# Spikes added inside TensorE's transposes, first tile pushed ahead, early norms on ScalarE

## The reference, cut to what matters

```python
h = layernorm(x) * (1 + ca) + sa
# per token: inp = r * wkv;  mem = 0.3*mem + inp - 0.05*(mem > 0.05);  spike = (mem - 0.05 > 0)
x = x + ga * spikes                       # "the sums"
h = layernorm(x) * (1 + cb) + sb          # 16 tiles of 128 tokens
for layer in range(2):                    # attention + MLP
    s = concat(h[:, :64], shift_by_one_token(h[:, 64:]))     # "shift_token"
    q, k, v = split(s @ wqkv[layer])
    q = q / max(norm(q), 1e-12) * q_scale   # per head, 8 heads of 64
    k = k / max(norm(k), 1e-12) * k_scale
    q, k = rotary(q), rotary(k)
    h = h + local_attention(q, k, v) @ wo[layer]             # window 64
    h = h + mlp(layernorm(shift_token(h)))
x = x + gb * h
```

## Time and profile before

| what | us |
|---|---|
| median of 3 runs | 548.56 (548.49 to 548.58) |
| profiled execution | 549.87, its span 548.1 |
| PE busy | 494.0 (90%) |
| DVE busy | 427.0 (78%) |
| ACT busy | 349.6 (64%) |
| POOL busy | 339.3 (62%) |

### The profile page before, as it was taken

One profiled execution on the slowest core, in us unless ns is written; L12 is line 12 of the kernel. 1 busy time (PEld: TensorE's weight loads), 2 busy tenths in 40 slices (PEclk: granted clock), 3 DMA queues, 4 the chain that ended last, 5 costly groups with the idle time before them and its releaser, 6 DMA issues.

```text
span 548.1 us, 11812 instructions
## 1 busy us (share of the span) xinstructions
PE 494.0 (90%) x4059; PEld 315.8 (58%) x4059; DVE 427.0 (78%) x1173; ACT 349.6 (64%) x1001; POOL 339.3 (62%) x271
## 2 busy tenths in 40 slices
PE   5844088999999999999899999999999999999996
PEld 5424033567777776443467777777544445667775
DVE  6999999899888976566889988995545687566665
ACT  5854007699999987534679999998556526533332
POOL 5990028999999998668989999994111277410000
PEclk9975579999999999999989999999999999999999
DMA  8600003211111112000221111111000000000000
GB/s 300 238 1 1 0 3 109 56 39 32 40 40 41 41 39 71 0 2 0 77 49 35 37 41 39 41 40 31 1 1 0 0 1 1 1 1 19 22 20 19
DMA packets 15025, 20.98 MB, mean 38 GB/s; under 512 B 2379, under 2 KB 9013, under 8 KB 14709
## 3 DMA queue, kind: packets, MB, share of 16 engines
q1 hardware_dynamic: 14676, 20.13, 13.3%
q10 hardware_dynamic: 288, 0.08, 0.1%
HBM read 9.99 MB, written 1.05 MB: 20 GB/s over the span
## 4 chain that ended last, share of the span: by engine, by line
PE 68%; DVE 18%; POOL 6%; issue 4%; ACT 3%; DMA 1%; DVEq 0%; SPq 0%; POOLq 0%; ACTq 0%
PE psT L1523 11%; PE psQK L1615 9%; PE psO L1738 6%; PE psO L1670 5%; PE psQK L1945 5%; PE psS L1718 5%; DVE vst L1108 3%; DVE vAB L1112 3%; PE psO L1523 3%; PE psS L2017 3%; PE psQK L1752 3%; PE psO L2017 2%; PE psQK L1877 2%; PE psS L1854 2%; PE psQK L1756 2%
## 5 line engine op out<-in xcount | busy, mean ns | idle before, releaser
L576 ACT ACTIVATE prob<-psS,nmx 128x128 f32<-128x128 f32 x256 | 90.1, 378 | 18.2 <-DVE nmx L1248 18.2
L904 POOL TENSOR_TENSOR rn<-ssq,half 128x16 f32<-128x16 f32 x32 | 93.2, 2913 | 8.6 <-DVE ssq L1234 8.5
L896 POOL TENSOR_TENSOR ra<-ra,rb 128x512 f32<-128x512 f32 x64 | 81.0, 1286 | 1.0 <-DVE rb L1216 0.8
L716 POOL TENSOR_TENSOR rst<-mv,half 128x4 f32<-128x4 f32 x24 | 25.7, 1072 | 73.8 <-DVE mv L1009 64.2
L1615 PE MATMUL psQK<-wqkv,hsA 128*128 128x512 f32 x128 | 62.0, 604 | 1.0 <-DVE hsA L1197 0.6
L576 ACT ACTIVATION_READ_ACCUMULATOR prob<-psS,nmx 128x1 f32 x256 | 55.4, 216 | 0.0
L912 POOL TENSOR_TENSOR qkn<-ra,rn 128x512 f32<-128x512 f32 x32 | 49.0, 1532 | 2.5
L1213 DVE TENSOR_TENSOR ra<-psQK,rope 128x512 f32<-128x512 f32 x64 | 43.9, 686 | 7.5 <-PE psQK L1615 6.6
L1216 DVE TENSOR_TENSOR rb<-psQK,rope 128x512 f32<-128x512 f32 x64 | 43.5, 680 | 0.0
L697 ACT ACTIVATE gel<-psQK 128x512 f32<-128x512 f32 x32 | 19.1, 597 | 37.5 <-PE psQK L1945 37.5
L1227 DVE TENSOR_REDUCE ssq<-sq 128x8 f32<-128x512 f32 x64 | 41.1, 676 | 1.6 <-ACT sq L516 1.3
(11 more groups left out here) (263 smaller groups left out, 1177.6 us busy)
## 6 DMA issues: line engine op xcount, KB each, us to landing
vAB<-vAB SPq DMA_DIRECT2D x62, 128.0 KB, 2.2
wqkv<-in_wqkv SPq DMA_DIRECT2D x2, 768.0 KB, 8.2
big<-in_x SPq DMA_DIRECT2D x4, 256.0 KB, 5.3
ra<-in_rope_t SPq DMA_DIRECT2D x1, 1024.0 KB, 7.7
ropeb<-in_rope SPq DMA_DIRECT2D x1, 1024.0 KB, 8.6
big<-in_ew SPq DMA_DIRECT2D x2, 512.0 KB, 4.1
wmod<-in_wmod SPq DMA_DIRECT2D x2, 384.0 KB, 6.8
out<-big SPq DMA_DIRECT2D x3, 256.0 KB, 2.3
```

The lines of the kernel that those rows point to most:

```text
L576: act.activation(prob[:, k, :], psS[:, hb, c * P:(c + 1) * P], ACT.Exp, bias=nmx[:, k:k + 1], accum_out=sums[:, n % 2, k:k + 1]).then_inc( ...
L896: pool.tensor_tensor(o, o, rb[:, r], ALU.add).then_inc(s["sum_" + name], 1)
L904: pool.tensor_tensor(rn[:, :], ssq[:, :], half[:, :], ALU.pow).then_inc(s["rn_ready"], 1)
```

## The change

1. Three currents on DVE: group 1's moves from POOL to DVE, before `quotient(3)`.
2. The spikes get a place of their own (`spikes = big[:, 6]`, where `x` had been loaded). PE transposes `x_cm` without them during the recurrence, and later adds the transposed spikes by a product with the identity into the same banks. `x_cm` itself gets them on POOL after the whole of layer 0's attention. The experts' weights, which go to the same place, are fetched at the start of layer 1.
3. In group 0 the first 128 tokens go ahead: one transpose, one scaling, two short copies. The other 384 tokens reach `hsA` by two transfers.
4. The inverse root of the first norm (group 0) and of attention tiles 0 and 1 is `exp(-0.5*ln(x))` on ACT; the activation table set is `natural_log_exp_and_others` for layer 0.
5. The lists of ACT, DVE, PE and POOL around it are reordered.

```diff
-                act.activation(rsg[:, gsl(g)] if g in (1, 2) else r_bank(g), ...
+                act.activation(rsg[:, gsl(g)] if g == 2 else r_bank(g), ...
+            act.preload_act_table_set("natural_log_exp_and_others")
             load_table(ACT.Exp)
...
+            def power(dst, src):
+                own.one(act.activation(dst, src, ACT.Ln, bias=0.0, scale=1.0))
+                return act.activation(dst, dst, ACT.Exp, bias=0.0, scale=-0.5)
+            def first_norm():
+                n = ln_no(1, 0)
+                act.wait_ge(s["ln_var"], n + 1)
+                power(rst[:, n % 4, :], mv[:, n % 4, :, 1]).then_inc(s["rst_act"], 1)
+                act.wait_ge(s["rst_act"], 1)
+                act.wait_ge(s["ln_rstd"], n + 1)
+                act.wait_ge(s["ln_t2"], n - 1)
+                for k in range(TPG):
+                    act.activation(lnx[:, n % 2, k, :], stat_bank(n)[:, k, :], ACT.Identity, ...).then_inc(s["ln_norm"], 1)
+                    if k == 1:
+                        act.wait_ge(s["first_t2"], 1)
+                        act.activation(z[:, 0:P], psQK[:, 0, 0:P], ACT.Identity, ...).then_inc(s["first_out"], 1)
+                act.wait_ge(s["ln_t2"], n + 1)
+                act.activation(z[:, P:GW], out_bank(n)[:, P:GW], ACT.Identity, ...).then_inc(s["ln_out"], 1)
+            def norms(n):
+                act.wait_ge(s["ssq_max"], n + 1)
+                if n:
+                    act.wait_ge(s["k_ready"], n)
+                    act.wait_ge(s["q_ready"], n)
+                power(rn[:, :], ssq[:, :]).then_inc(s["rn_ready"], 1)
-            ln_norm(ln_no(1, 0))
-            stack_out(0)
+            first_norm()
             ln_norm(ln_no(1, 1))
+            squares_k(0)
             ln_norm(ln_no(1, 2))
             stack_out(1)
-            squares_k(0)
             squares_q(0)
+            norms(0)
             ln_norm(ln_no(1, 3))
...  (ACT, tile -2: after k_turned)
+                    if n == 1 - LEAD:
+                        norms(1)
...  (POOL)
-            current(1)
             current(2)
-            add_spikes(2)
-            ln_rstd(ln_no(1, 0))
-            add_spikes(3)
-            for g in range(1, NG):
-                ln_rstd(ln_no(1, g))
+            n = ln_no(1, 0)
+            pool.wait_ge(s["rst_act"], 1)
+            pool.tensor_tensor(nmr[:, n % 4, :], nmean[:, n % 4, :], rst[:, n % 4, :], ALU.mult).then_inc(s["ln_rstd"], 1)
+            ln_rstd(ln_no(1, 1))
+            ln_rstd(ln_no(1, 2))
...
-                    norms(n + 2)
+                    if n + 2 > 1:
+                        norms(n + 2)
...
                     rope_sum(n + 3, 1)
+                    if n + 3 == 0:
+                        ln_rstd(ln_no(1, 3))
                     rope_sum(n + 3, 0)
...
                 if l == 0:
+                    pool.wait_ge(s["spikes"], 2)
+                    for g in range(NG):
+                        pool.tensor_tensor(x_cm[:, gsl(g)], x_cm[:, gsl(g)], spikes[:, gsl(g)], ALU.add).then_inc(s["x_mixed"], 1)
                     phase_scalars()
                     phase_whole()
...  (DVE)
             current(0)
+            current(1)
             quotient(3)
             current(3)
...
-            add_spikes(0)
-            add_spikes(1)
+            dve.memset(cend[:, 0, 0:1], 0.0).then_inc(s["spikes"], 1)
+            dve.tensor_scalar(by_chunk(spikes, NG - 1), of_group(ph, NG - 1, 1), -1.0, ...).then_inc(s["spikes"], 1)
             ln(ln_no(1, 0))
-            threshold(Steps(dve, s["spk"]), 3)
             ln(ln_no(1, 1))
-            ln(ln_no(1, 2))
...
-            dve.wait_ge(s["ln_out"], ln_no(1, 0) + 1)
-            shifted(hsA, z, 0, "hsA_ready")
+            dve.wait_ge(s["first_out"], 1)
+            dve.tensor_copy(hsA[0:64, 0:P], z[0:64, 0:P]).then_inc(s["hsA_first"], 1)
+            dve.tensor_copy(hsA[64:128, 1:P + 1], z[64:128, 0:P]).then_inc(s["hsA_first"], 1)
+            ln(ln_no(1, 2))
+            dve.wait_ge(s["rope_ready"], 4)
+            rope_products(0, 1)
             ln(ln_no(1, 3))
-            dve.wait_ge(s["rope_ready"], 4)
-            qk_first(0)
+            rope_products(0, 0)
+            sum_squares(0, 1)
+            sum_squares(0, 0)
+            clamped(0)
             rope_products(1, 1)
+            q_normed(0)
             rope_products(1, 0)
-            q_normed(0)
...  (PE)
+            for g in range(NG):
+                for k in range(TPG):
+                    mm(stat_flat(ln_no(1, g))[:, k * P:(k + 1) * P], x_cm[...], ident[:, :],
+                       is_transpose=True, start=(k == 0), stop=(k == TPG - 1), skip_group_check=True)
...
             def stack_t1(g):
-                pe.wait_ge(s["x_mixed"], g + 1)
-                four(stat_flat(ln_no(1, g)), lambda k: x_cm[...]).then_inc(s["ln_t1"], 1)
+                pe.wait_ge(s["spikes"], 1 + (g == NG - 1))
+                for k in range(TPG):
+                    i = mm(stat_flat(ln_no(1, g))[:, k * P:(k + 1) * P], spikes[...], ident[:, :],
+                           start=False, stop=(k == TPG - 1), skip_group_check=True)
+                i.then_inc(s["ln_t1"], 1)
             stack_t1(0)
             stack_t1(1)
             stack_t1(2)
-            keep_clock(10, psT1[:, :])
-            ln_t2(ln_no(1, 0))
             stack_t1(3)
+            keep_clock(2, psT1[:, :])
+            first = ln_no(1, 0)
+            pe.wait_ge(s["ln_norm"], TPG * first + 1)
+            pe.transpose(psQK[:, 0, 0:P], lnx[:, first % 2, 0, :], ident[:, :]).then_inc(s["first_t2"], 1)
             keep_clock(4, psT1[:, :])
             pe.wait_ge(s["ld_wq"], 16)
             pe.wait_ge(s["edges"], 4)
             proj_part(0, 0, 1)
+            pe.wait_ge(s["ln_norm"], TPG * (first + 1))
+            for k in range(1, TPG):
+                i = pe.transpose(out_bank(first)[...], lnx[:, first % 2, k, :], ident[:, :])
+            i.then_inc(s["ln_t2"], 1)
+            proj_part(0, 0, 0)
             ln_t2(ln_no(1, 1))
-            proj_part(0, 0, 0)
+            proj_part(0, 1, 1)
             ln_t2(ln_no(1, 2))
-            proj_qk(0, 1)
+            proj_part(0, 1, 0)
             keep_clock(4, psT1[:, :])
...  (SP)
+                    sp.wait_ge(s["ln_out"], ln_no(1, 0) + 1)
+                    sp.dma_start(hsA[0:64, P:GW], z[0:64, P:GW]).then_inc(s["hsA_dma0"], 16)
+                    sp.dma_start(hsA[64:128, P + 1:GW + 1], z[64:128, P:GW]).then_inc(s["hsA_dma0"], 16)
+                else:
                     sp.wait_ge(s["x_mixed"], NG)
                     sp.dma_start(ew1, a["ew1"]).then_inc(s["ld_ew"], 16)
                     sp.dma_start(ew2, a["ew2"]).then_inc(s["ld_ew"], 16)
```

More of the change, by code:

```diff
@@ L128, in program @@
         seed, rsg = ek, sab
+        spikes = big[:, 6, :]
         oT = big[:, 0:4, :]
@@ L189, in program @@
         names = """ld_id ld_x0 ld_x1 ld_x2 ld_x3 ld_wm0 ld_wm1 ld_ew ld_c ld_wr ld_wa ld_wq ld_wl ld_lru ld_rt ld_moe ld_out st_out
-            init table edges mod_raw cnt_ready cnt_sum renewed spk hsA_dma1 hsA_dma2 hsA_dma3 silu_c mod_mm mod_fin sc_ready
+            init table edges mod_raw cnt_ready cnt_sum renewed spikes hsA_dma0 hsA_dma1 hsA_dma2 hsA_dma3 silu_c mod_mm mod_fin sc_ready
             ln_t1 ln_var ln_rstd ln_norm ln_t2 ln_out
@@ L463, in receptance @@
                 act.wait_ge(s["num_ready"], min(g + 2, NG))
-                act.activation(rsg[:, gsl(g)] if g in (1, 2) else r_bank(g), r_bank(g), ACT.Sigmoid, bias=vec[:, V_BR:V_BR + 1]).then_inc(s["r_ready"], 1)
+                act.activation(rsg[:, gsl(g)] if g == 2 else r_bank(g), r_bank(g), ACT.Sigmoid, bias=vec[:, V_BR:V_BR + 1]).then_inc(s["r_ready"], 1)
             act.preload_act_table_set("natural_log_exp_and_others")
@@ L543, in v_copy @@
                 elif n == 0:
-                    act.wait_ge(s["x_mixed"], NG)
+                    act.wait_ge(s["spikes"], 2)
                 act.activation(vB[:, u, :], psO[:, 1, :], ACT.Copy).then_inc(s["v_evac"], 1)
@@ L1147, in threshold @@
             def threshold(steps, g):
-                steps.did(dve.tensor_scalar(by_chunk(ekv, g), of_group(ph, g, 1), -1.0, mod[:, 0, GA, bof(g):bof(g) + 1],
+                steps.did(dve.tensor_scalar(by_chunk(spikes, g), of_group(ph, g, 1), -1.0, mod[:, 0, GA, bof(g):bof(g) + 1],
                                             ALU.is_lt, ALU.mult))
+            dve.wait_ge(s["xT_evac"], NG)
             threshold(own, 0)
@@ L1590, in _ @@
                 mixer_turn(g)
-            pe.wait_ge(s["cur_vec"], 2)
+            pe.wait_ge(s["cur_vec"], 3)
             for n in range(4):
@@ L1601, in stacked @@
                 g = i // TPG
-                if l == 0 and g or g == NG - 1:
+                if l == 0 and i == 0:
+                    pe.wait_ge(s["hsA_first"], 2)
+                elif l == 0 or g == NG - 1:
                     pe.wait_ge(s[f"hsA_dma{g}"], 32 * (l + 1))
                 else:
-                    pe.wait_ge(s["hsA_ready"], 2 * (l + g + 1))
```

(18 more changed lines are left out.)

30 lines of the change are left out of this document (16 added, 14 removed).

## The result

The changed kernel takes 551.92 us (median of 5, 551.13 to 553.63) against 548.49 (548.44 to 548.58) for the kernel before: ratio 1.007 [1.005, 1.009]. It is 3.4 us slower. The prediction said 548.6 and a range up to 550.4.

A forecast was written before the change was run, and what follows sets the result against it. PE was taken to bound the kernel nearly alone from 111.94 us, so the opening's savings count in full. Terms +0.15 + 0 - 1.75 + 1.3 + 0.3 + 0 = 0.0 gave a median of 548.6 us, range 546.4 to 550.4.

The forecast's parts named there:

- Parts 1 to 4, the front: Opening: +0.15 for currents, 0 for sums on TensorE, -1.75 for first norms and first tile; that gain between 0.6 and 2.9.
- The first projection's own terms: Opening: normalising, wait, scaling, copies and hand-overs put at 1.7 us after ACT's start at 80.85, so first projection at 82.55.
- Part 1: Opening, three currents on DVE: recurrence starts between 0.15 us earlier and 0.7 later; +0.15 taken.
- Part 3: Opening, first tile ahead: first projection 3.35 us earlier, mostly lost again in ACT's queue; tile 0's scores 1.1 earlier.
- Part 2, the price at layer 0's end, the power: Layer 0's end: four POOL sums make its power 3.46 us late, less 2.16 of cover: +1.3, bounds 0 to 3.1.
- Part 2, the phases that meet DVE's copies: Layer 0's end: two DVE copies held up beside POOL's phases, 0 to 0.8 us; +0.3 taken.
- Part 2, weights fetched later: Layer 1's start: 1 MB ahead of v's transfers lands them some 4.5 us later, within the slack: 0, up to +0.7.
- The base: Whole kernel: difference worked out to the profiled execution (549.87 us, 1.31 above the median) and put on the median 548.56.
- Rival A: Layer 1's start: half clock near 273 us may not come again, -1.7 less 0.5: 546.9 to 547.2; chance 0.20.
- C: Layer 0's end: longer POOL sums and fully held copies cost 3.1 us instead of 1.6: 550.1; chance 0.12.
- D: Opening: PE's idle time between 84.5 and 87.4 brings a fall of its clock, costing 1.7 us: 550.3; chance 0.06.
- E: Layer 0: squares, copies or exponentials need another table set, at least two loads: 551.5 or more; with the unknown 0.04.

The follow-up runs named there:

- e5: Changed kernel with POOL's four sums in its idle stretches of the opening and the experts' weights fetched in the middle of layer 0's attention: 547.20 us, ratio 0.997.
- e12: Kernel of e5 with the experts' weights fetched at layer 1's start again, nothing else: 549.25 us, ratio 1.0015.
- e11: Kernel of e5 with the whole first group going ahead instead of its first 128 tokens: 548.90 us, ratio 1.0007.
- e7: Kernel before with the experts' weights fetched at layer 1's start, nothing else: 551.53 us, ratio 1.0043.
- e9: Kernel of e5 with the current of group 1 back on POOL: 547.78 us, ratio 0.9978.
- e10: Kernel of e5 with the first layer norm's inverse root back on POOL: 548.78 us, ratio 1.0004.
- e2: Changed kernel with POOL's four sums moved from the end of layer 0's attention into its MLP: 553.74 us, ratio 1.0095.
- e4: Changed kernel with 12 more clock-keeping products on PE behind the first projections: 554.77 us, ratio 1.0118.
- e8: Changed kernel with the norms of attention tiles 0 and 1 back on POOL: 554.32 us, ratio 1.0095.
- e1: Changed kernel with the experts' weights fetched after layer 1's fifth tile instead of ahead of its first v transfers: 549.96 us, ratio 1.0022.
- e6: Kernel before with four 128x512 additions on POOL ahead of the phases at layer 0's end: 551.89 us, ratio 1.0053.

## Why the prediction was wrong

The sum was 0.0. By medians it is -1.4 + 2.7 + 2.0 = +3.3, against 3.4 measured (e5 against before; the changed kernel against e12; e12 against e5).

- **Parts 1 to 4, the front.** Predicted -1.6 in all (+0.15, 0, -1.75); measured -1.5 in the rows and -1.4 in the medians. Most places were right to 0.15, in part by luck. The first projection's own terms (0.4, 0.35, 0.4, 0.35 and twice 0.3) add up to 2.1 and not 1.7; the trace has 82.61 - 80.62 = 1.99, and ACT started 0.23 earlier than predicted, since the first statistics came at 78.14 and not at 78.4 to 78.6. The terms of ACT's queue behind 84.6 add up to 92.5 and not 92.15. Part 1 was +0.15; the recurrence started 0.05 earlier, which is nothing to tell from zero. The quotient fell to 1.22 once POOL was free. Part 3 was right for the whole but wrong in its reason: "mostly lost again" held the first tile ahead to be worth little by itself. e11 shows 1.27 at group 3's normalising and 1.7 in the median, since without it ACT's queue has a hole of 2.19.
- **Part 2, the price at layer 0's end, the power.** Predicted 1.3, measured 1.44 in the trace. The mechanism and size were right: POOL at 216.46 is 3.51 late against the shifted 214.45.
- **Part 2, the phases that meet DVE's copies.** This term failed in size. I took 0.3 and called the copies "not on PE's path at once"; the copy of 222.55 cost 1.08. Its statistics, the next layer norm and the residual stand behind it. The bound was wrong as well: two copies at 1.24 in place of 0.43 cost 1.62 in full and not 0.8, so the rule that the prediction weighed there, taken in full, would have added 1.3 and not 0.5; the trace gave 0.8 more. One copy of the two was held, and it paid what was left of the POOL instruction, not a share of its own length. Power and copy together are 2.5 in the rows, 2.7 between the changed kernel and e12.
- **Part 2, weights fetched later.** This is the step that was furthest out: "about 0. I take 0, up to +0.7", measured 2.0. I had v land 4.5 later, and it did so by 4.1: issued 1.19 later (against 272.26 + 1.06, the shift of tile 16), landed 6.4 after its issue instead of 3.5. What failed is the slack. By the prediction's own numbers 4.5 against 7.5 - 3.3 = 4.2 already left 0.3, which it rounded to 0. And I read 7.5 us between issue and use, in an execution where the granted clock was 0.50 for 3.4 us in between the earlier trace rows. Without that fall the way from the turning to the weighing is 5.03 (e5), not 6.51: 1.5 less slack. So the slack was 7.5 - 3.5 - 1.5 = 2.5, and 4.1 - 2.5 = 1.6 is the wait of 1.56.
- **The base.** For the same reason the difference must not be put on the median as it stands. The profiled execution held 1.3 us that most executions of before, 548.4 to 548.9, seem not to hold; e7's profile and the pair of e5 and e9 speak for it. Rival A took the fall's absence for a gain; against such a median there was nothing to gain. Its stated price also gives 548.56 - 1.7 + 0.5 = 547.4 and not 546.9 to 547.2.
- **The rivals.** C named the place and 550.1; POOL cost 2.5 where C gave 3.1. D's fall in the opening did not come in the profile after (granted 1.00 from 84 to 88), and came in e9 (0.60 from 88 to 92), e10 and e11. E fell: ACT loads 13 tables in both kernels, and ln and exp took 0.20 each. Nobody had the slower side from the weights.

What stays open: the changed kernel's other executions are 0.7 to 2.5 above the profiled one. e7 and e12 show that the weights' place alone brings such a spread, and one execution of e12 shows a way; but e2 and e4 lost more in the median than their profiles explain, e8's further loss is a longer wait and a fall of the clock without a known cause, and no run here separates these.

## What to carry to other kernels

Read the slack of a transfer at the full granted clock; if a stretch of half clock lies in it, take that out first, and ask whether the profiled execution is typical before its difference goes on the median. When work is taken off a path, look where the same engine has idle stretches as long as the work: here the sums fitted into POOL's gaps a few us later, and the same change went from +3.4 to -1.4. For every POOL sum or product that is moved, list the DVE copies and clamps on SBUF that it and the work behind it will now meet, and charge each that is on the path with what is left of the POOL instruction. Before reading tenths between two profiles, look how far equal programs differ.

## What the runs showed of the hardware

A DVE copy, or an operation with one tensor on SBUF, can be held to the end of a POOL instruction, be it of 4 columns or of 512: 0.17 became 1.12, 1.16 and 1.18 beside sums of 1.27, a copy of 0.23 became 1.18, one of 0.42 became 1.51 beside a POOL product of 2.35. DVE instructions that read PSUM kept their length beside the same sums (0.88 or 0.89 for the statistics at 82.5 with and without one).

POOL's power did not hold them. In e5 two copies of 128 columns ran at their own length inside a power:

```profile
81.24 1.02 POOL L756 TENSOR_TENSOR rst<-mv,half 128x4 f32<-128x4 f32 x1 [0.73 <-DVE mv L1054]
...
81.96 0.22 DVE L1312 COPY hsA<-z 64x128 f32<-64x128 f32 x1 [0.80 <-ACT z L547]
```

In the kernel before, two copies of 512 columns beside a power (84.66 to 85.80) took 0.42 and 0.43. So not every POOL instruction holds a copy. Whether its kind or its size decides, no run here separates.

The Trainium skill, GPSIMD Engine Reference, "Specifications", names contention for a two-port mode or for two SBUF inputs; the trace agrees that there is one, and the held clamps and copies have one SBUF tensor as input.

The same wait of PE, 1.88 us at the start of layer 1, (1.87 in some) was followed by a granted clock of about half in before, e1, e4, e6 and e9, and by 1.00 in the changed kernel, e5 and e7. In these eight PE had been busy without a pause for the 6.8 us ahead of it. Such a stretch can't be priced from one profile.
